# Query and key stacks turned by DMA instead of TensorE, the attention's early steps moved forward in the hand-written order, and the output bias added later

## Chip, cores and metric

One core of one Trainium2 chip. The metric is the device time of one launch in microseconds (us), median over runs. Engines: PE (TensorE), DVE (VectorE), ACT (ScalarE), POOL (GpSimd), SP (SyncE, which issues every DMA of this kernel).

## What is computed

A vision-tower layer on x of shape 8 x 512 x 256 x 4, float32:

```
h = einsum('bhid,oi,od->bho', x, weighted_sum, weight)     # token mixing: 8 x 512 x 256
q, k, v = split(layernorm(h) @ qkv_w.T + qkv_b)            # 16 heads of 16
q, k = unit(rotate(q)), unit(rotate(k))                    # rotary, then each head's row over its norm
h = h + softmax(q k' / 4) v @ out_w.T + out_b
p = sigmoid(layernorm(h) @ Wg + bg); w = p * (p > 0.5)     # 8 experts, each of 256 -> 1024 -> 256
h = h + sum_e w_e * (relu(layernorm(h) @ W1_e + b1_e) @ W2_e + b2_e)
```

## The kernel before

Eight batches of 512 tokens (four tiles of 128) run one after the other. The attention of batch 0 runs **alone**; then the experts (FFN) of batch b are **merged** with the attention of batch b+1, for b = 0 (where the expert weights are also split into two float16 parts and written to DRAM) and in a loop over b = 1 to 6; the experts of batch 7 end the program.

**FFN chunks.** An expert has 8 chunks of 128 hidden units, 64 chunks in all. Chunk c on PE is `f1 c` (6 matmuls of 128x512 into one of two PSUM banks, line 859) and, three chunks later (LAG), `f2 c` (12 matmuls of 128x256, lines 878 to 881). Between them ACT applies the ReLU twice (lines 666, 669), POOL forms the low part (line 549). `f1 n` waits for ACT's chunk n-2. After an expert's last `f2` DVE adds the result into `acc` (line 1091, "acc"); the next expert's first `f2` waits for that (line 874), since it reuses the banks.

**Order.** Each engine runs one fixed list, in order. `attention_order` (lines 56 to 88) gives every attention step a place counted in chunks, and `merge` (lines 112 to 133) puts the steps between the `f1` and `f2` of the chunks. The same step name is run by all the engines that have a part in it, so the place orders PE, ACT, DVE and POOL alike. In a chunk c the steps placed below c + 0.5 come after `f1 c`, then comes `f2 c-3` (and "acc" after an expert's last one), then the steps placed below c + 1.

**Attention steps** per tile t: `split` (x into two parts, ACT and DVE), `mix` (24 matmuls), `ln1`, `ln1_turn`, `qkv` (12 matmuls; DVE copies out with the bias, lines 963, 964), `rotate` (ACT squares at line 618, POOL at line 556, DVE at lines 976 to 982), `qk_norm` (DVE, 12 small operations per half, lines 989 and 894 to 901), `unit` (DVE, line 996), `stack` and `qk_turn`; then `scores`, `weigh` and the rest.

`stack t` writes the unit queries and keys as float16 high and low parts into one buffer `stack` (128 partitions x 2 x 1024): ACT the high (line 624), DVE the low (line 1005), for a = 0 (queries) and 1 (keys). `qk_turn t` transposes it on PE, 8 blocks of 128x128 for each a (line 761), into PSUM; ACT copies that into `qt` and `kt` (`take_turned`, line 588, traced at line 581, inside the next tile's `stack`). As there is one buffer, `stack t+1` on ACT and DVE waits until tile t has been turned (lines 622, 1004).

**SP's queue** is one list too. For expert e of batch b (`load_expert`, lines 489 to 496): wait for `f1` of expert e-2 to be done, load w1s (1 MB); wait for `f2` of expert e-2 to be done, load w2s (1 MB). For e = 3 the second wait is for `f2 15`:

```
wait(sp, f2_done, b, HM * (e - 1))
sp.dma_start(w2s[s][:], w2_parts[e]).then_inc(w2_in[s].sem, 16)
```

**The output bias** is added to `resid` by POOL (line 569) after the last `qkv`; `project`, after all scores, waits for it.

Of the kernel before, what the change touches and what calls it, by code (L numbers as in the profile page):

```python
# [26 lines left out]
P = 128  # L27
# [28 lines left out]
def attention_order(alone=False):  # L56
# [3 lines left out]
    for t in range(TT):  # L60
        steps += [(MIX[t - 1] - 0.05 if t else 0.3, "split", t), (MIX[t], "mix", t),
                  (9.0 + 1.5 * t, "ln1_turn", t), (10.55 + 1.5 * t, "qkv", t), (10.6 + 1.5 * t, "rotate", t),
                  (17.1 + 1.5 * t, "unit", t), (18.6 + 1.5 * t, "stack", t), (20 + 1.5 * t, "qk_turn", t)]
    steps += [(6.8, "ln1", 0), (14.7, "qk_norm", 0), (19.2, "qk_norm", 1)]
    if alone:

        order = ["ln1_turn 0", "ln1_turn 1", "qkv 0", "rotate 0", "ln1_turn 2", "qkv 1", "rotate 1", "qk_norm 0",
                 "unit 0", "ln1_turn 3", "qkv 2", "stack 0", "rotate 2", "unit 1", "qkv 3", "qk_turn 0", "stack 1",
                 "rotate 3", "qk_norm 1", "qk_turn 1", "unit 2", "stack 2", "unit 3", "qk_turn 2", "stack 3",
                 "qk_turn 3"]  # L70
        places = {name: 8 + 0.1 * k for k, name in enumerate(order)}
        steps = [(places.get(f"{stage} {n}", at), stage, n) for at, stage, n in steps]
# [19 lines left out]
MIX = [2.1, 3.5, 4.9, 6.3]  # L92
# [104 lines left out]
def build(nc, x_t, mix_w, mix_sum_t, qkv_w_t, qkv_b, out_w_t, out_b, gate_w, gate_b, w1, b1_t, w2, b2,  # L197
# [5 lines left out]
    with ExitStack() as ctx:  # L203
# [14 lines left out]
        ident16 = sb("ident16", [P, P], F16)  # L218
# [122 lines left out]
        stack_turned = signal("stack_turned", 2 * TT)  # L341
        qt_out = signal("qt_out", TT)
        kt_out = signal("kt_out", TT)
# [101 lines left out]
        def _(sp):  # L445
# [90 lines left out]
            with sp.Fori(1, BATCHES - 2) as i:  # L536
                body(i, True, True)
# [5 lines left out]
        def _(pool):  # L543
            def steps(stage, n, fb, ab):
# [21 lines left out]
                elif stage == "qkv" and n == TT - 1:  # L566
# [8 lines left out]
            pool.tensor_copy(ident16[:], ident[:]).then_inc(pool_consts, 1)  # L575
# [3 lines left out]
        def _(act):  # L579
            def copy(out_ap, in_ap):  # L580
                return act.activation(out_ap, in_ap, ACT.Copy)  # L581

            def take_turned(t, a, b, alone):

                dst, done = ((qt, qt_out), (kt, kt_out))[a]
                wait(act, stack_turned, b, 2 * t + a + 1)
                wait(act, scored, b, 0)
                copy(dst[:, :, t * P:(t + 1) * P], qk_turn_bank(a, alone)).then_inc(done.sem, 1)
# [9 lines left out]
            def steps(stage, n, fb, ab):  # L598
# [87 lines left out]
        def _(pe):  # L686
# [17 lines left out]
            def steps(stage, n, fb, ab):  # L704
# [46 lines left out]
                elif stage == "qk_turn":  # L751
                    if fb is not None:
                        wait(pe, qkv_out, ab, 2 * TT)
                    if n == 0 and fb is None:
                        pe.wait_ge(pool_consts, 2)
                    for a in range(2):
                        wait(pe, stack_ready, ab, 2 * n + a + 1)
                        wait(pe, (qt_out, kt_out)[a], ab, n)
                        turned = qk_turn_bank(a, fb is None)
                        for h in range(HEADS // 2):  # L760
                            last = pe.transpose(turned[:, h, :],  # L761
                                                stack[:, a, 2 * h:2 * h + 2, :, :].rearrange("p h s d -> p (h s d)"),
                                                ident16[:])
                        last.then_inc(stack_turned.sem, 1)
# [125 lines left out]
        def _(dve):  # L890
# [23 lines left out]
            def steps(stage, n, fb, ab):  # L914
# [281 lines left out]
```

## Time and profile before

| | us |
|---|---|
| median of 3 runs (lowest, highest) | 2021.08 (2020.14, 2027.73) |
| profiled execution: its own time, its span | 2029.17, 2027.4 |
| one turn of the merged loop (start of one f1 0 to the next) | 237.7 |
| experts of batch 7 alone, to the end | 173.3 |
| PE busy | 1911.6 (94%) |
| DVE, ACT, POOL busy | 792.3, 1142.6, 678.6 |

A row of a timeline has start, duration, engine, line, operation, output <- input, and in brackets the idle time of the engine before it and what ended that. Matmuls overlap, so starts tell their rate better than durations.

### The profile page before, as it was taken

To read this page: it belongs to the slowest core of one execution; us is meant where nothing else is said; L and a number is where in the kernel's file an instruction comes from. 1 tells how busy PE (TensorE), PEld (TensorE's weight loads), DVE (VectorE), ACT (ScalarE), POOL (GpSimd) and SP (SyncE) were. 2 spreads that over 40 slices of the span, in tenths; PEclk is the share of its full clock that TensorE was granted. 3 is DMA by queue.
4 is the path that set the end of the run, shared out by engine and by line. 5 is a ranking of instruction groups with operands and counts; after the bars stand their busy time and mean duration, and the time that the engine had idled before them with its cause. 6 is when DMAs were issued, how large, how long until landed. Compare 5 with 4: busy or idle time off the path is not lost.

```text
span 2027.4 us, 36619 instructions
## 1 busy us (share of the span) xinstructions
PE 1911.6 (94%) x13152; PEld 1211.9 (60%) x13152; DVE 792.3 (39%) x1660; ACT 1142.6 (56%) x1969; POOL 678.6 (33%) x570
## 2 busy tenths in 40 slices
PE   5679888899999999999999999999999999999999
PEld 4246543577547764567646675467655776456666
DVE  6756933547203380145602472133810456013000
ACT  2644666544765457644765447654576446754444
POOL 1103422324323242333423343232423334233443
PEclk8779999999999999999999999999999999999999
DMA  4113332332112221131212312122221322113221
GB/s 154 38 53 113 105 130 84 123 138 84 63 64 105 97 83 63 66 130 67 84 63 87 113 66 81 63 105 95 72 75 63 109 91 84 63 63 103 104 96 53
DMA packets 40461, 176.92 MB, mean 87 GB/s; under 512 B 4056, under 2 KB 17120, under 8 KB 23904
## 3 DMA queue, kind: packets, MB, share of 16 engines
q1 hardware_dynamic: 40288, 174.52, 24.2%
q8 instruction: 120, 1.97, 0.4%
q14 instruction: 53, 0.43, 0.1%
HBM read 153.54 MB, written 20.97 MB: 86 GB/s over the span
## 4 chain that ended last, share of the span: by engine, by line
PE 77%; issue 7%; DVE 7%; ACT 2%; POOL 1%; ACTq 0%; DVEq 0%; POOLq 0%
PE bank_h L859 28%; PE bank_f L878 10%; PE bank_f L880 10%; PE bank_f L881 10%; PE bank_o L788 5%; PE bank_s L776 3%; PE bank_s L692 2%; PE bank_s L693 2%; PE bank_s L694 2%; DVE tmp_b L976 1%; PE bank_s L761 1%; POOL hl L549 1%; DVE y L899 1%; PE bank_s L842 1%; ACT hh L669 1%
## 5 line engine op out<-in xcount | busy, mean ns | idle before, releaser
L549 POOL TENSOR_TENSOR hl<-h,hh 128x512 f16<-128x512 f32 x512 | 608.4, 1189 | 1148.2 <-ACT hh L669 670.7
L859 PE MATMUL bank_h<-x,w1s 128*128 128x512 f16 x3072 | 756.0, 383 | 19.5 <-issue 9.1
L666 ACT ACTIVATE h<-bank_h,b1s 128x512 f32<-128x512 f32 x512 | 353.5, 690 | 468.6 <-PE bank_h L859 452.7
L878 PE MATMUL bank_f<-w2s,hh 128*128 128x256 f16 x2048 | 563.2, 275 | 2.1 <-DVE acc L1091 1.3
L880 PE MATMUL bank_f<-w2s,hh 128*128 128x256 f16 x2048 | 561.1, 274 | 0.0
L881 PE MATMUL bank_f<-w2s,hl 128*128 128x256 f16 x2048 | 560.9, 274 | 0.0
L859 PEld LDWEIGHTS bank_h<-x,w1s 128*128 128x128 f16 x3072 | 287.6, 99 | 345.7 <-issue 49.9
L669 ACT ACTIVATE hh<-bank_h,b1s 128x512 f16<-128x512 f32 x512 | 352.7, 689 | 0.0
L636 ACT ACTIVATE probs<-bank_s 128x512 f32<-128x512 f32 x480 | 262.3, 604 | 153.7 <-PE bank_s L776 153.6
L878 PEld LDWEIGHTS bank_f<-w2s,hh 128*128 128x128 f16 x2048 | 202.2, 99 | 113.8 <-issue 41.0
L1091 DVE SCALAR_TENSOR_TENSOR acc<-bank_f,gw,acc 128x256 f32<-128x256 f32 x256 | 106.1, 476 | 349.9 <-PE bank_f L881 349.8
L880 PEld LDWEIGHTS bank_f<-w2s,hh 128*128 128x128 f16 x2048 | 201.6, 98 | 48.7 <-issue 0.8
L881 PEld LDWEIGHTS bank_f<-w2s,hl 128*128 128x128 f16 x2048 | 201.4, 98 | 24.4
L1009 DVE RECIPROCAL rc<-bank_m 128x16 f32<-128x16 f32 x32 | 8.2, 257 | 402.6 <-PE bank_m L798 402.6
L788 PE MATMUL bank_o<-probs,v 128*32 128x512 f32 x1024 | 137.2, 608 | 1.2 <-ACT probs L636 0.6
L776 PE MATMUL bank_s<-qt,kt 64*128 64x512 f16 x480 | 98.8, 392 | 15.0 <-ACT probs L636 13.6
L692 PE MATMUL bank_s<-mix,xh 128*128 128x256 f32 x256 | 78.0, 305 | 16.5 <-DVE xl L922 16.4
L776 PEld LDWEIGHTS bank_s<-qt,kt 64*128 64x128 f16 x480 | 24.4, 93 | 101.5 <-ACT probs L636 51.1
L922 DVE TENSOR_TENSOR xl<-xraw,xh 128x512 fp32r<-128x512 f32 x64 | 48.7, 772 | 83.3 <-ACT xh L581 83.3
L618 ACT ACTIVATE probs<-qk 128x512 f32<-128x512 f32 x32 | 20.2, 630 | 104.0 <-DVE qk L963 104.0
L556 POOL TENSOR_TENSOR tmp_a<-qk,cos 128x512 f32<-128x512 f32 x32 | 42.4, 1326 | 96.6 <-DVE qk L963 96.6
L693 PE MATMUL bank_s<-mix,xh 128*128 128x256 f32 x256 | 74.0, 289 | 0.0
(137 smaller groups left out, 1788.8 us busy)
## 6 DMA issues: line engine op xcount, KB each, us to landing
w1s<-w_parts SPq DMA_DIRECT2D x56, 1024.0 KB, 4.8
w2s<-w_parts SPq DMA_DIRECT2D x56, 1024.0 KB, 4.8
xraw<-in_x_t_dram SPq DMA_DIRECT2D x32, 512.0 KB, 4.1
raw<-in_w_dram SPq DMA_DIRECT2D x16, 1024.0 KB, 6.4
w_parts<-w1s SPq DMA_DIRECT2D x8, 1024.0 KB, 8.8
w_parts<-w2s SPq DMA_DIRECT2D x8, 1024.0 KB, 10.7
out_dram<-acc SPq DMA_DIRECT2D x16, 256.0 KB, 6.1
raw<-in_qkv_w_t_dram SPq DMA_DIRECT2D x1, 768.0 KB, 6.8
```

The source lines that it names most:

```text
L549: pool.tensor_tensor(hl[n % HBUFS][:], h32[n % 2][:], hh[n % HBUFS][:], ALU.subtract)\
L636: act.activation(probs[u % 2][:, 2 * half + j, :], score_bank(2 * n + j, fb is None)[:, :], ACT.Exp, scale=SCORE_SCALE).then_inc(exped.sem, 1)
L666: act.activation(h32[n % 2][:], bank_h[n % 2][:, :], ACT.Relu, bias=b1s[:, e, m:m + 1]).then_inc(h_hi.sem, 1)
L669: act.activation(hh[n % HBUFS][:], bank_h[n % 2][:, :], ACT.Relu, bias=b1s[:, e, m:m + 1]).then_inc(h_hi.sem, 1)
L692: pe.matmul(out_ap, high[k], w[k], start=start and k == 0, stop=False, skip_group_check=True)
L693: pe.matmul(out_ap, high[k], lo_w[k], start=False, stop=False, skip_group_check=True)
L776: pe.matmul(score_bank(2 * n + j, fb is None)[:, :], kt[lo:lo + 64, h // 2, tile * P:(tile + 1) * P], qt[lo:lo + 64, h // 2, :], start=Tru ...
L788: last = pe.matmul(bank_o[32 * j:32 * j + 32, :], v1[:, tile, h, :, :].rearrange("p s d -> p (s d)"), probs[n % 2][:, j, :], start=(tile = ...
L859: last = pe.matmul(bank_h[n % 2][:, :], w[:, wp, k, m * P:(m + 1) * P], x16[:, xp, k, :], start=(k == 0 and wp + xp == 0), stop=(k == DK - ...
L878: pe.matmul(o, high, w[:, 0, m, :], start=(m == 0 and t % 2 == 0), stop=False, skip_group_check=True)
L880: pe.matmul(o, high, w[:, 1, m, :], start=False, stop=False, skip_group_check=True)
L881: last = pe.matmul(o, low, w[:, 0, m, :], start=False, stop=(m == HM - 1), skip_group_check=True)
```

## The change

1. `qk_turn`, `take_turned`, `ident16` and the signals `qt_out` and `kt_out` are gone. SP issues eight DMA transposes per batch instead (`turn_stacks`), each from one half of `stack` (128 x 1024 float16, 256 KB) into 128 columns of `qt` or `kt`, after `stack_ready`. `stack_turned` becomes one semaphore for each of a = 0 and 1, raised by the DMA. In SP's list they come after `load_expert(b, 3)`; for batch 1 ahead of `load_raw(4)`; for batch 0 ahead of `load_raw(1)`.
2. Places: `mix` and `split` of tiles 1 to 3 1.1 chunks earlier, `ln1` to `rotate` 1.1, `qk_norm` 1.8 and 3.5, `unit` 1.9, `stack` 2.0. `scores` stays at 25.6.
3. The output bias is a step of its own at 23.5.
4. SP's loop over batches is unrolled.

```
-                  (9.0 + 1.5 * t, "ln1_turn", t), (10.55 + 1.5 * t, "qkv", t), (10.6 + 1.5 * t, "rotate", t),
-                  (17.1 + 1.5 * t, "unit", t), (18.6 + 1.5 * t, "stack", t), (20 + 1.5 * t, "qk_turn", t)]
-    steps += [(6.8, "ln1", 0), (14.7, "qk_norm", 0), (19.2, "qk_norm", 1)]
+                  (7.9 + 1.5 * t, "ln1_turn", t), (9.45 + 1.5 * t, "qkv", t), (9.5 + 1.5 * t, "rotate", t),
+                  (15.2 + 1.5 * t, "unit", t), (16.6 + 1.5 * t, "stack", t)]
+    steps += [(5.7, "ln1", 0), (12.9, "qk_norm", 0), (15.7, "qk_norm", 1), (23.5, "out_bias", 0)]
...
-MIX = [2.1, 3.5, 4.9, 6.3]
+MIX = [1.0, 2.4, 3.8, 5.2]
...
+            def turn_stacks(b, tiles):
+                for t in tiles:
+                    for a in range(2):
+                        wait(sp, stack_ready, b, 2 * t + a + 1)
+                        if t == 0:
+                            wait(sp, scored, b, 0)
+                        sp.dma_start_transpose((qt, kt)[a][:, :, t * P:(t + 1) * P],
+                                               stack[:, a].rearrange("p h s d -> p (h s d)"))\
+                          .then_inc(stack_turned[a].sem, 16)
...
             load_x(1, [0, 1])
+            turn_stacks(0, range(TT))
             load_raw(1)
...
             for e in range(2, EXPERTS):
+                if e == 3:
+                    turn_stacks(1, range(TT))
                 if e + 1 < EXPERTS:
                     load_raw(e + 1)
...
                 for e in range(2, EXPERTS):
                     load_expert(b, e)
+                    if more and e == 3:
+                        turn_stacks(b + 1, range(TT))
...
-            with sp.Fori(1, BATCHES - 2) as i:
+            for i in range(1, BATCHES - 2):
                 body(i, True, True)
...
-                elif stage == "qkv" and n == TT - 1:
+                elif stage == "out_bias":
                     wait(pool, ln1_out, ab, TT)
                     pool.tensor_tensor(resid[:], resid[:], outb[:].unsqueeze(1).broadcast_to([P, TT, D]),
...
                 elif stage == "stack":
                     wait(act, qk_unit, ab, n + 1)
                     for a in range(2):
-                        wait(act, stack_turned, ab, 2 * (n - 1) + a + 1)
+                        wait(act, stack_turned[a], ab, 16 * n)
                         high, _, unit_qk = stack_slots(n, a)
                         copy(high, unit_qk).then_inc(stack_hi.sem, 1)
-                        if n:
-                            take_turned(n - 1, a, ab, fb is None)
...
                         wait(dve, stack_hi, ab, 2 * n + a + 1)
-                        wait(dve, stack_turned, ab, 2 * (n - 1) + a + 1)
+                        wait(dve, stack_turned[a], ab, 16 * n)
                         dve.tensor_tensor(low, unit_qk, high, ALU.subtract).then_inc(stack_ready.sem, 1)
```

## Rows read from the trace of the kernel before

**Rows 1.** Stages: us, each engine's busy us (instructions), granted clock (PEclk), DMA share, GB/s.
```profile
903.00:1140.60 237.60, 233.30 (x1646) 148.07 (x1645) 88.25 (x191) 138.47 (x242) 83.57 (x69) 1.00 0.23 83
...
940.00:965.00 25.00, 25.00 (x165) 18.34 (x164) 16.87 (x26) 11.46 (x21) 12.21 (x10) 1.00 0.13 52
...
218.00:222.00 4.00, 1.66 (x4) 0.58 (x5) 3.97 (x6) 2.94 (x5) 2.90 (x3) 0.72 0.05 20
```

**Rows 2.** Waits of PE in one turn of the merged loop: total, times, longest.
```profile
PE bank_h L859 <- ACT hh L669: 1.0, 1, 1.0
PE bank_s L761 <- issue: 0.5, 1, 0.5
PE bank_s L692 <- DVE xl L922: 0.5, 1, 0.5
```

**Rows 3.** The chain of waits in that turn: start, us, what.
```profile
980.06 1.30 PE bank_h L859 x6
981.36 0.89 PE bank_s L761 x16
```

**Rows 4.** ACT's copies of the turned keys: busy, mean ns | idle.
```profile
L581 ACT ACTIVATE kt<-bank_s 128x1024 f16<-128x1024 f16 x28 | 29.5, 1054 | 0.0
```

**Rows 5.** Timeline in that turn: the bias on POOL, and what ran beside and after it.
```profile
967.13 2.34 POOL L569 TENSOR_TENSOR resid<-resid,outb 128x1024 f32<-128x1024 f32 x1
...
967.25 2.30 DVE L899 SCALAR_TENSOR_TENSOR y<-y 128x64 f32<-128x64 f32 x1
...
970.11 0.22 DVE L899 SCALAR_TENSOR_TENSOR y<-y 128x64 f32<-128x64 f32 x1
...
974.23 1.47 PE L859 MATMUL bank_h<-x,w1s 128*128 128x512 f16 x6 [1.03 <-ACT hh L669]
```

**Rows 6.** PE at the start of that turn: three f1, then the first mix.
```profile
908.18 4.37 PE L859 MATMUL bank_h<-x,w1s 128*128 128x512 f16 x18 [1.81 <-issue]
913.05 0.36 PE L692 MATMUL bank_s<-mix,xh 128*128 128x256 f32 x1 [0.50 <-DVE xl L922]
```

**Rows 7.** SP's issues and PE around f2 15.
```profile
977.04 0.32 SPq L496 DMA_DIRECT2D w2s<-w_parts  x1
...
978.45 0.28 PE L878 MATMUL bank_f<-w2s,hh 128*128 128x256 f16 x1
```

**Rows 8.** DVE in that turn, from tile 2's qkv to the second qk_norm.
```profile
960.67 0.69 DVE L963 TENSOR_TENSOR qk<-bank_s,qkvb 128x512 f32<-128x512 f32 x1 [1.27 <-PE bank_s L694]
...
976.56 1.05 DVE L996 TENSOR_TENSOR probs<-qk,y 128x512 f32<-128x512 f32 x1
977.53 1.65 DVE L1091 SCALAR_TENSOR_TENSOR acc<-bank_f,gw,acc 128x256 f32<-128x256 f32 x4
...
980.90 1.19 DVE L989 TENSOR_SCALAR ss<-ss 128x64 f32<-128x64 f32 x1
...
985.91 1.29 DVE L1005 TENSOR_TENSOR stack<-probs,stack 128x512 f16<-128x512 f32 x2
```

**Rows 9.** DMA issues by line: times, KB each, us to landing (first row: 976 to 984 us alone).
```profile
w2s<-w_parts SPq DMA_DIRECT2D x1, 1024.0 KB, 4.7
...
w_parts<-w2s SPq DMA_DIRECT2D x8, 1024.0 KB, 10.7
```

**Rows 10.** Landing times of the DMAs of L476, of L480 and of L502.
```profile
DMA to landing us min/median/max: 4.7/4.8/6.0
...
DMA to landing us min/median/max: 6.7/6.8/7.5
...
DMA to landing us min/median/max: 2.1/6.1/7.6
```

**Rows 11.** Timeline of batch 0's attention, alone: the last stack and the first scores.
```profile
72.08 0.63 ACT L581 ACTIVATE stack<-probs 128x512 f16<-128x512 f32 x1 [0.45 <-DVE probs L996]
...
77.36 0.61 PE L776 MATMUL bank_s<-qt,kt 64*128 64x512 f16 x2 [1.16 <-issue]
```

**Rows 12.** PE's timeline with batch 0's experts: the first f1 after a gap.
```profile
220.34 2.74 PE L859 MATMUL bank_h<-x,w1s 128*128 128x512 f16 x6 [2.81 <-ACT hh L669]
```

More of the change, by code:

```diff
@@ L61, in attention_order @@
         steps += [(MIX[t - 1] - 0.05 if t else 0.3, "split", t), (MIX[t], "mix", t),
-                  (9.0 + 1.5 * t, "ln1_turn", t), (10.55 + 1.5 * t, "qkv", t), (10.6 + 1.5 * t, "rotate", t),
-                  (17.1 + 1.5 * t, "unit", t), (18.6 + 1.5 * t, "stack", t), (20 + 1.5 * t, "qk_turn", t)]
-    steps += [(6.8, "ln1", 0), (14.7, "qk_norm", 0), (19.2, "qk_norm", 1)]
+                  (7.9 + 1.5 * t, "ln1_turn", t), (9.45 + 1.5 * t, "qkv", t), (9.5 + 1.5 * t, "rotate", t),
+                  (15.2 + 1.5 * t, "unit", t), (16.6 + 1.5 * t, "stack", t)]
+    steps += [(5.7, "ln1", 0), (12.9, "qk_norm", 0), (15.7, "qk_norm", 1), (23.5, "out_bias", 0)]
     if alone:
         order = ["ln1_turn 0", "ln1_turn 1", "qkv 0", "rotate 0", "ln1_turn 2", "qkv 1", "rotate 1", "qk_norm 0",
-                 "unit 0", "ln1_turn 3", "qkv 2", "stack 0", "rotate 2", "unit 1", "qkv 3", "qk_turn 0", "stack 1",
-                 "rotate 3", "qk_norm 1", "qk_turn 1", "unit 2", "stack 2", "unit 3", "qk_turn 2", "stack 3",
-                 "qk_turn 3"]
+                 "unit 0", "ln1_turn 3", "qkv 2", "stack 0", "rotate 2", "unit 1", "qkv 3", "stack 1",
+                 "rotate 3", "qk_norm 1", "unit 2", "stack 2", "unit 3", "stack 3"]
         places = {name: 8 + 0.1 * k for k, name in enumerate(order)}
@@ L217, in build @@
         ident = sb("ident", [P, P])
-        ident16 = sb("ident16", [P, P], F16)
         mix = sb("mix", [P, 2, XK, D], F32R)
@@ L340, in build @@
         stack_ready = signal("stack_ready", 2 * TT)
-        stack_turned = signal("stack_turned", 2 * TT)
-        qt_out = signal("qt_out", TT)
-        kt_out = signal("kt_out", TT)
+        stack_turned = [signal(f"stack_turned{a}", 16 * TT) for a in range(2)]
         scored = signal("scored", 4 * UNITS)
@@ L387, in qkv_banks @@
             return bank_h if alone and t % 2 else bank_s
-        def qk_turn_bank(a, alone):
-            return (bank_f if alone else bank_s)[a][:, :].bitcast(F16).rearrange("p (h t) -> p h t", t=P)
         def stack_slots(t, a):
@@ L574, in _ @@
             pool.wait_ge(consts_in, 16 * 9)
-            pool.tensor_copy(ident16[:], ident[:]).then_inc(pool_consts, 1)
             run(pool, steps)
@@ L581, in copy @@
                 return act.activation(out_ap, in_ap, ACT.Copy)
[L583 to L588, printed above, removed]
             def split_x(b, t):
@@ L621, in steps @@
                     for a in range(2):
-                        wait(act, stack_turned, ab, 2 * (n - 1) + a + 1)
+                        wait(act, stack_turned[a], ab, 16 * n)
                         high, _, unit_qk = stack_slots(n, a)
                         copy(high, unit_qk).then_inc(stack_hi.sem, 1)
-                        if n:
-                            take_turned(n - 1, a, ab, fb is None)
-                elif stage == "qk_turn" and n == TT - 1:
-                    for a in range(2):
-                        take_turned(n, a, ab, fb is None)
                 elif stage == "scores":
@@ L750, in steps @@
                     last.then_inc(qkv_done.sem, 1)
[L751 to L764, printed above, removed]
                 elif stage == "scores":
@@ L767, in steps @@
                     if n == 0:
-                        wait(pe, qt_out, ab, TT)
-                        wait(pe, kt_out, ab, TT)
+                        for turned in stack_turned:
+                            wait(pe, turned, ab, 16 * TT)
                         wait(pe, qkv_out, ab, 2 * TT)
@@ L783, in steps @@
                         wait(pe, ln1_lo, ab, TT)
+                        if fb is None:
+                            pe.wait_ge(pool_consts, 1)
                     if tile == 0:
```

## The prediction, made before the changed kernel ran

> **What bounds the kernel now.** I read the stages first. In a turn of the merged loop PE is busy 233.3 of 237.6 us at the full granted clock (PEclk 1.00 is the level of 2.4 GHz), DVE, ACT and POOL for 88, 138 and 84 [rows 1]. So PE's own work is the turn, and an edit there pays in two ways only: work that leaves PE, or a wait of PE that appears or goes. The waits of PE come next: beside the start of a turn they are 1.0 us for ACT's ReLU, 0.5 at the first turning on PE and 0.5 for the split of x [rows 2]. From 940 to 965 us PE never waits [rows 1]. An engine off PE matters only where PE's next instruction stands behind it, and so the lists of DVE, ACT and SP around `f2 15` decide this change.
>
> **The turnings on PE.** The 16 blocks of a tile take 0.89 us in the chain of waits, an `f1` 1.30 [rows 3]. Four tiles: 3.6 us, and the 0.5 us wait before one of them [rows 2]: -4.1 us a turn.
>
> **ACT's copies.** 8 per batch of 1.05 us [rows 4] go. PE waits for none of them [rows 2], so I cost this at 0.
>
> **The bias.** POOL's addition takes 2.34 us, and beside it one small DVE operation takes 2.30 us where the same operation 3 us later takes 0.22 [rows 5]. DVE thus loses 2.1 us inside `qk_norm 0`, behind it stand DVE's `qkv 3` copy, ACT's square and ReLU, and PE's `f1 18` waits 1.03 us for that ReLU [rows 5, 2]. At 23.5 DVE has nothing beside it but the end of `stack 3`. On POOL it then stands before chunk 24's `hl`, which `f2 24` needs three chunks later; that cover is 3 x 2.6 us against 2.34. Without it 2 us would come back. -1.0 us a turn.
>
> **`mix` earlier.** Now PE runs three `f1` and then waits 0.5 us for the split of x [rows 6]. In the new order `mix 0` stands after two, while the split still follows ACT's first ReLU, so it is ready at the same time: PE waits one `f1` longer, +1.3 us a turn. Later `mix` steps have a chunk of slack, and I see no wait of PE in which the 1.3 could vanish. `split 1` passes ACT's second ReLU, which `f1 3` needs only after `mix 1`: 0. Bounds 0 and 1.8 (all of the wait).
>
> **`ln1` to `rotate` earlier.** PE has no wait there [rows 1] and the order among these steps stays, so 0. One neighbour changes: DVE's accumulate after `f2 7` now follows `rotate 0`; I count about 1 us of slack before `f2 8`. If it is gone, 1 us.
>
> **The new wait.** Call the end of `f2 15` E. Before, SP issues w2s right behind it (977.04, so E is about 976.85), and `f2 16` starts at E + 1.6, after `f1 19` [rows 7]. The places give this new list in chunk 18: `f1 18`, `stack 1`, `unit 2`, then `f2 15` and its accumulate. Before, the accumulate came ahead of `stack 0`. So on DVE the accumulate for which `f2 16` waits now stands behind `stack 1`, and `stack 1` on ACT and DVE waits until tile 0 has been turned. SP issues those DMAs only after the wait of `load_expert(b, 3)` for `f2 15`, and behind its 1 MB. No edge goes round in a circle, but the chain is: end of `f2 15`, w2s, two turned stacks, ACT, DVE, `f2 16`.
> - Is tile 0's stack ready by then? Before, DVE runs from tile 2's `qkv` copy (960.67) to `unit 0` (976.56) without much rest, 15.9 us [rows 8]. New: 15.9 - 2.1 (bias) + 1.05 (`unit 0`) + 5.0 (`qk_norm 1`, from 980.90 to 985.91, now ahead of `stack 0`) + 1.3 (the two low parts) = 21.2 us. PE from the same point to E: 16.2 before; three half chunks more (3.9) and 1.0 of waiting less give 19.1. So the stack is ready at E + 2, and w2s, which lands 4.7 us after its issue [rows 9], at E + 4.9. The transfers come behind it in the same queue.
> - One turned stack is 256 KB. The trace has no such DMA. Lower end: the plain rate; the shortest store of 256 KB (L502) lands after 2.1 us [rows 10] and w2s with four times as much after 4.7, so (4.7 - 2.1) / 3 = 0.9 us for each 256 KB more. Upper end: the slowest large DMA, 10.7 us [rows 9]. Between: the loads of L476 and L480 both move 1 MB, in 256 runs of 4 KB and 1024 runs of 1 KB by their code, and land after 4.8 and 6.8 us [rows 10]; 768 runs more cost 2.0 us. A stack cut into blocks of 128 columns is 1024 runs of 256 bytes, the stored 256 KB are 256 runs of 1 KB. So 0.9 + 2.0 = 2.9 us, an estimate, and I take it: these loads are the rows nearest in what a turning multiplies, the runs.
> - The two stacks land at E + 7.8 and E + 10.7. Then ACT's copy 0.63 [rows 11], DVE's low part 0.65, `unit 2` 1.05, half of the accumulate 0.8 [rows 8]: `f2 16` at E + 13.8, against E + 1.6: +12.2 us. At 0.9 us a stack it is +8.2.
> - Behind it: after an idle of 2.81 us one `f1` takes 2.74 us instead of the 1.46 of one without a gap [rows 12, 5] and that stage has a granted clock of 0.72 [rows 1], which is part of it spent at 1.2 GHz. +1.3 us.
> - Later tiles: a pair every 5.8 us (2 x 2.9) lands tile 3 at E + 28.1; PE gets to `scores 0` after 7 chunks of 2.6 us and the stall, E + 30.4. No further wait. What SP holds back meanwhile, w1s of expert 4, is needed 8 chunks after its old issue: 0. SP's unrolled loop and PE's wait at `weigh`: 0, both wait for others anyway.
>
> The Trainium skill prices the stack twice. *DMA: Bandwidth & Descriptors*, section Latency and other measured facts, gives a DMA transpose 261 GB/s; that makes 1.0 us a stack, an estimate, and a sum of about 2058. *VectorE: DVE Perf Modes*, section The three transpose paths, gives 1309 ns for one 128x128 block by DMA against 390 for TensorE; eight blocks in a row would be 10.5 us, an estimate, and the sum that of the slow rival below. The trace's 16 blocks in 0.89 us [rows 3] are 56 ns each on PE, far below the page's 390, and no run here shows the DMA yet.
>
> **The sum.** A turn: +12.2 + 1.3 + 1.3 - 4.1 - 1.0 = +9.7, six turns: +58. Batch 1's attention has no w2s ahead of its DMAs but the same accumulate behind `stack 1`, and DVE is busier there; it also loses the bias's wait and the gap that follows (2.81 and 1.28 us [rows 12]): I put +2 (-4 to +12). Batch 0: tiles 2 and 3 follow each other at once, 5.3 us from the last stack to the scores [rows 11]; two landings of about 4 us in place of PE and ACT: +5 (0 to 12). In all +65. The profiled execution took 2029.2 us, 8 above the median of the three runs; the turns are alike in both, so I add to the median: 2021 + 65 = **2086**.
>
> **Rivals.**
> - *Short transfers* (0.9 us a stack): +5.7 a turn, and +1 in all outside the turns: 2021 + 34 + 1 = 2056. For it: the same bytes as any copy. Against: the run count.
> - *Slow transfers.* A stack takes as long as the slowest large DMA, 10.7 us [rows 9]. Then pairs are what the batch waits for: tile 3 lands at E + 4.9 + 8 x 10.7 = E + 90 where `scores 0` stood at E + 18: +72, less 4 saved, seven batches, and some 40 us more in batch 0: about 2540. From about 5 us a stack on (pairs at 10 us, +26 a turn at `scores`) it passes 2200. For it: nothing in the trace; against it: the rows from which I took 2.9.
> - *No stall, so faster.* The place is the accumulate after `f2 15`. If the second stack lands by E + 2.3, `f2 16` is late by less than the 3.8 us that the rest of a turn gains (4.1 + 1.0 - 1.3), and if it lands early enough nothing is lost: 2021 - 6 x 3.8 - 5 = 1993, or 1985 if the `mix` wait is absorbed too. It needs DVE to have `stack 0` ready before `f2 15` and the DMAs not to queue behind w2s. For it: w2s could be overtaken, and PE's work does fall by 4.1. Against it: SP's own order, which I read from the code.
> - *Given back evenly.* The DMAs don't wait for w2s and are short: the second stack lands 2.1 us after it is ready, at E + 4.1, `f2 16` is 5.6 late, less 5.1, and with or without the `mix` wait it ends between 2011 and 2031.
>
> **Chances.** The forecast's case (1.5 to 5 us a stack) 0.45, short 0.18, slow (over 5) 0.12, given back 0.11, faster 0.14. Slower by over 0.5% (10 us, about what a measurement of this kernel can tell): 0.45 + 0.18 + 0.12 = 0.75; within it 0.11; faster 0.14. The range of 2005 to 2200 leaves out the slow rival's upper part (0.10) and most of the faster case (0.10).
>
> **What would show it.** Right: in the waits of PE a wait of 8 us or more, once a turn, at L878 for DVE's accumulate or for `stack`; DVE's low part of `stack 1` waiting for a DMA into `qt` or `kt`; landing times that start behind w2s; PE busy down by 4 us a turn, the bias beside no DVE operation, 1.8 us before `mix 0`. Wrong: the turn below 237 us with no such wait; a wait at `scores` or in ACT's ReLU as the largest; or transfers of other than 1.5 to 5 us each.

## The result, and the profile after

The changed kernel takes 2071.73 us (median of 4 runs, 2066.59 to 2073.78), the kernel before 2024.07 beside it (4 runs): a ratio of 1.0232, 95% interval 1.0209 to 1.0255. The forecast was 2086, with 0.75 for slower: the direction and the range held, and the rise came out at 47.7 us where the working had 65.

The profiled executions span 2070.3 and 2027.4 us. DVE's copy of x marks the start of each turn: from the second copy to the eighth it was 430.5 to 1853.9 us before and is 433.1 to 1896.9 now. So the six turns hold 40.4 of the 42.9 us (237.2 us a turn became 244.0), what lies ahead of them 2.6, the last experts nothing.

In the changed kernel `f1` is L842, `f2` L861 to L864, the mix L687, the scores L757, the accumulate L1074, the split of x L905, the stack's copy L588 (ACT) and low part L988 (DVE), `unit` L979, the transposes L497. First the windows, as in [rows 1]: two turns, and three short stretches inside turns.

```profile
675.80:918.50 242.70, 230.02 (x1582) 145.34 (x1580) 83.14 (x192) 131.97 (x234) 83.03 (x69) 0.99 0.28 90
918.50:1163.50 245.00, 232.18 (x1582) 146.73 (x1580) 82.99 (x191) 132.08 (x234) 82.73 (x69) 0.97 0.27 89
685.00:689.00 4.00, 3.66 (x28) 3.29 (x29) 1.49 (x3) 1.16 (x2) 0.00 (x0) 1.00 0.46 142
928.00:932.00 4.00, 3.93 (x23) 3.96 (x24) 1.22 (x2) 0.63 (x1) 0.00 (x0) 0.67 0.48 136
1003.70:1008.00 4.30, 4.30 (x17) 2.46 (x18) 2.68 (x5) 1.26 (x2) 0.27 (x1) 0.52 0.54 122
```

PE runs 64 instructions fewer in a turn (the turnings), and is idle 12.7 us of it where it was 4.3 [rows 1]. Its busy time falls from 233.3 to 230.0 in one turn and only to 232.2 in the other, by the granted clock: 0.99 against 0.97. The waits of PE in the first of these turns, to be read against [rows 2]:

```profile
PE bank_f L861 <- DVE acc L1074: 8.6, 1, 8.6
PE bank_s L687 <- DVE xl L905: 2.1, 1, 2.1
PE bank_h L842 <- issue: 1.9, 1, 1.9
```

The last line was there before. The 1.0 us for the ReLU behind the bias and the 0.5 at the first turning are gone, the 0.5 before the mix is 2.1, and one wait is new: `f2 16` for DVE's accumulate. The timeline of the next turn around that wait, the stretch of [rows 7, 8]; a line of dots stands for rows left out:

```profile
993.48 1.46 PE L842 MATMUL bank_h<-x,w1s 128*128 128x512 f16 x6
...
993.68 0.32 SPq L488 DMA_DIRECT2D w2s<-w_parts  x1
...
993.96 2.13 DVE L988 TENSOR_TENSOR stack<-probs,stack 128x512 f16<-128x512 f32 x2
995.52 1.24 SPq L497 DMA_TRANSPOSE qt<-stack  x1
996.02 0.68 DVE L979 TENSOR_TENSOR probs<-qk,y 128x512 f32<-128x512 f32 x1
996.86 2.01 SPq L497 DMA_TRANSPOSE kt<-stack  x1
999.98 0.63 ACT L588 ACTIVATE stack<-probs 128x512 f16<-128x512 f32 x1 [6.34 <-DMA qt<-stack]
1000.80 1.43 DVE L988 TENSOR_TENSOR stack<-probs,stack 128x512 f16<-128x512 f32 x2 [4.10 <-ACT stack L588]
1000.87 0.63 ACT L588 ACTIVATE stack<-probs 128x512 f16<-128x512 f32 x1 [0.27 <-DMA kt<-stack]
...
1001.52 1.23 SPq L497 DMA_TRANSPOSE qt<-stack  x1
...
1002.14 0.68 DVE L979 TENSOR_TENSOR probs<-qk,y 128x512 f32<-128x512 f32 x1
1002.74 1.65 DVE L1074 SCALAR_TENSOR_TENSOR acc<-bank_f,gw,acc 128x256 f32<-128x256 f32 x4
...
1003.67 0.40 PE L861 MATMUL bank_f<-w2s,hh 128*128 128x256 f16 x1 [8.73 <-DVE acc L1074]
```

Read it from the bottom. `f2 16` starts when DVE has accumulated half of `f2 15`; DVE stands first at `stack 1`, which waits 4.10 us for ACT, and ACT waited 6.34 us for the first transpose of tile 0 to land; SP issued that one behind w2s. `f2 15` ended at E = 993.5, so `f2 16` is at E + 10.2, and then runs at 0.52 of the full clock for 4.3 us (window above). The DMA view of the whole run:

```profile
DMA packets 108038, 193.59 MB, mean 94 GB/s; under 512 B 71640, under 2 KB 84704, under 8 KB 91488
...
w2s<-w_parts SPq DMA_DIRECT2D x56, 1024.0 KB, 4.8
qt<-stack SPq DMA_TRANSPOSE x32, 2.7
kt<-stack SPq DMA_TRANSPOSE x32, 2.8
```

A transpose of 256 KB lands 2.7 to 2.8 us after its issue (median), 4.5 and 4.0 us in the stretch above, behind w2s.

### The profile page after: what moved, and what is told of

It is laid out like the page before. It is cut to its first block, busy times and chain, and to the rows that moved or that the text cites. A ratio compares the mean times of both kernels' runs of the same rounds, so it can differ in the third digit from the quotient of the medians.

```text
span 2070.3 us, 35350 instructions
## 1 busy us (share of the span) xinstructions
PE 1890.8 (91%) x12640; PEld 1190.9 (58%) x12640; DVE 758.5 (37%) x1660; ACT 1089.7 (53%) x1905; POOL 671.4 (32%) x569
## 2 busy tenths in 40 slices
DMA packets 108038, 193.59 MB, mean 94 GB/s; under 512 B 71640, under 2 KB 84704, under 8 KB 91488
## 4 chain that ended last, share of the span: by engine, by line
PE 78%; DVE 6%; issue 6%; ACT 2%; POOL 1%; DMA 1%; SPq 0%; DVEq 0%; ACTq 0%; POOLq 0%
PE bank_h L842 29%; PE bank_f L861 10%; PE bank_f L863 10%; PE bank_f L864 10%; PE bank_o L771 5%; PE bank_s L757 3%; PE bank_s L687 3%; PE bank_s L689 3%; PE bank_s L688 3%; DMA kt<-stack 1%; ACT hh L664 1%; PE bank_s L825 1%; POOL hl L557 1%; PE bank_m L781 1%; DVE qk L964 1%
## 5 line engine op out<-in xcount | busy, mean ns | idle before, releaser
L557 POOL TENSOR_TENSOR hl<-h,hh 128x512 f16<-128x512 f32 x512 | 600.4, 1173 | 1236.1 <-ACT hh L664 669.1
L842 PE MATMUL bank_h<-x,w1s 128*128 128x512 f16 x3072 | 762.1, 386 | 11.9 <-issue 9.8
L861 PE MATMUL bank_f<-w2s,hh 128*128 128x256 f16 x2048 | 567.2, 277 | 64.8 <-DVE acc L1074 64.0
L863 PE MATMUL bank_f<-w2s,hh 128*128 128x256 f16 x2048 | 565.4, 276 | 0.0
L864 PE MATMUL bank_f<-w2s,hl 128*128 128x256 f16 x2048 | 565.1, 276 | 0.0
L842 PEld LDWEIGHTS bank_h<-x,w1s 128*128 128x128 f16 x3072 | 290.8, 99 | 339.1 <-issue 58.3
L861 PEld LDWEIGHTS bank_f<-w2s,hh 128*128 128x128 f16 x2048 | 203.2, 99 | 179.4 <-DVE acc L1074 55.2
L1074 DVE SCALAR_TENSOR_TENSOR acc<-bank_f,gw,acc 128x256 f32<-128x256 f32 x256 | 106.1, 477 | 365.0 <-PE bank_f L864 364.9
L863 PEld LDWEIGHTS bank_f<-w2s,hh 128*128 128x128 f16 x2048 | 202.6, 99 | 51.9 <-issue 0.8
L864 PEld LDWEIGHTS bank_f<-w2s,hl 128*128 128x128 f16 x2048 | 202.6, 99 | 25.9
L757 PE MATMUL bank_s<-qt,kt 64*128 64x512 f16 x480 | 98.0, 393 | 34.1 <-DMA kt<-stack 22.3
L687 PE MATMUL bank_s<-mix,xh 128*128 128x256 f32 x256 | 81.3, 318 | 28.8 <-DVE xl L905 28.8
L757 PEld LDWEIGHTS bank_s<-qt,kt 64*128 64x128 f16 x480 | 24.0, 93 | 120.5 <-issue 70.0
L588 ACT ACTIVATE stack<-probs 128x512 f16<-128x512 f32 x64 | 38.5, 627 | 90.2 <-DMA qt<-stack 56.2
L905 DVE TENSOR_TENSOR xl<-xraw,xh 128x512 fp32r<-128x512 f32 x64 | 50.9, 807 | 87.7 <-ACT xh L588 87.6
L988 DVE TENSOR_TENSOR stack<-probs,stack 128x512 f16<-128x512 f32 x64 | 55.4, 888 | 69.4 <-ACT stack L588 68.3
L689 PE MATMUL bank_s<-mix,xl 128*128 128x256 f32 x256 | 77.3, 302 | 0.0
```

The lines of the kernel that those rows point to most:

```text
L557: pool.tensor_tensor(hl[n % HBUFS][:], h32[n % 2][:], hh[n % HBUFS][:], ALU.subtract)\
L687: pe.matmul(out_ap, high[k], w[k], start=start and k == 0, stop=False, skip_group_check=True)
L689: last = pe.matmul(out_ap, low[k], w[k], start=False, stop=stop and k == n - 1, skip_group_check=True)
L757: pe.matmul(score_bank(2 * n + j, fb is None)[:, :], kt[lo:lo + 64, h // 2, tile * P:(tile + 1) * P], qt[lo:lo + 64, h // 2, :], start=Tru ...
L842: last = pe.matmul(bank_h[n % 2][:, :], w[:, wp, k, m * P:(m + 1) * P], x16[:, xp, k, :], start=(k == 0 and wp + xp == 0), stop=(k == DK - ...
L861: pe.matmul(o, high, w[:, 0, m, :], start=(m == 0 and t % 2 == 0), stop=False, skip_group_check=True)
```

## The experiments

The theory: the time is lost at `f2 16`, because tile 1's stack waits for tile 0's transposes ahead of the accumulate, and a little at the mix. Rivals: the transposes themselves are slow or disturb the weights; or the order costs the same without them. Ratios are to the kernel before, timed beside each; they stand as recorded, and a quotient of two medians differs from them by up to 0.002.

### The parts of the change, undone one at a time

**The mix back by a chunk.**

```diff
-MIX = [1.0, 2.4, 3.8, 5.2]
+MIX = [2.0, 3.1, 4.2, 5.2]
```

> The changed kernel with one edit: the mixes stand at 2.0, 3.1, 4.2 and 5.2, so that the first again follows three f1 instead of two, while the last keeps its new place. Theory (the changed kernel's added time is the accumulate of expert 1 held behind stack 1, plus PE's longer wait at the first mix, plus lost clock): PE's wait at L687 for the split falls from 2.1 to 0.5 us a turn and the stage's granted clock stays at 1.00, so 1.6 us a turn and up to 0.9 more where the clock fell; with batch 1, 10 to 18 us less than the changed kernel, a ratio to the kernel before of 1.015 to 1.019 where the changed kernel has 1.023. Rival (the time of the first mix is absorbed by PE's longer wait later): no difference, 1.022 to 1.025.

Ratio 1.0153 (1.0134 to 1.0172), a turn of 242.1 us. PE's waits in a turn of this kernel:

```profile
PE bank_f L861 <- DVE acc L1074: 8.7, 1, 8.7
...
PE bank_s L687 <- DVE xl L905: 0.5, 1, 0.5
```

The mix waits 0.5 us again, and the large wait is untouched. So the mix's place costs 1.8 us a turn, 1.6 of it waiting. Behind the mix the granted clock now stays at 1.00 in all six turns, where it fell in four; but PE's busy time falls by only 0.3 us a turn (231.6 to 231.3), since the slow stretch behind `f2 16` remains.

**The stacks two chunks apart.**

```diff
-                  (15.2 + 1.5 * t, "unit", t), (16.6 + 1.5 * t, "stack", t)]
+                  ([15.2, 16.7, 18.6, 20.7][t], "unit", t), ([16.6, 18.55, 20.6, 22.6][t], "stack", t)]
```

> The changed kernel with one edit: stack 1 and unit 2 move from 18.1 and 18.2 to 18.55 and 18.6, behind f2 15 and its accumulate on DVE, and the later units and stacks are spread out (unit 3 at 20.7, stacks 2 and 3 at 20.6 and 22.6). Theory (the accumulate waits behind stack 1, which waits for the turned tile): f2 16 then waits only for DVE's backlog, about 2.7 us instead of 8.7, with some 1 to 3 us of new waits at f1 21 to f1 24 for ACT, which still waits for the tiles; with less clock lost about 4 to 6 us a turn less, ratio 1.004 to 1.012. Rival (the wait for the turned tile itself costs the time, wherever it stands, as ACT and its ReLU stand behind it too): the waits move to f1 and the ratio stays within 1.018 to 1.026.

Ratio 1.0045 (1.0029 to 1.0060), a turn of 237.8 us. In a turn of this kernel the wait shrinks from 8.7 to 2.6 us, and little new appears (0.9 us for the ReLU in three of the six turns):

```profile
PE bank_f L861 <- DVE acc L1074: 2.6, 1, 2.6
```

With the accumulate ahead of `stack 1` most of the loss is gone, and every transpose is still there. So the transfers as such cost little; what costs is that the accumulate stands behind `stack 1`. Whether that is the wait for the landing or DVE's own work there, this run does not separate, as both moved; the second buffer below does.

**Tile 0's transposes ahead of w2s** on SP:

```diff
+                if e == 3 and b + 1 < BATCHES:
+                    turn_stacks(b + 1, [0])
...
-                        turn_stacks(b + 1, range(TT))
+                        turn_stacks(b + 1, range(1, TT))
```

> The changed kernel with one edit: SP issues tile 0's two transposes after w1s of expert 3 and ahead of its wait for f2 15 and of w2s; the other tiles stay. Theory (DVE's backlog makes tile 0's stack ready only 2 us after f2 15, and w2s in front adds the rest): the two land 2.7 us after they are issued instead of 4.5 and 4.0, so stack 1 and with it the accumulate come about 1.3 us earlier, f2 16 waits some 7.4 us; 1 to 2 us a turn less, ratio 1.016 to 1.021. Rival (the queue behind w2s is most of the wait): f2 16 waits under 5 us, ratio below 1.012.

Ratio 1.0164 (1.0141 to 1.0187); in a turn of this kernel (`f2` is L863) the wait is 7.5 us instead of 8.6 or 8.7:

```profile
PE bank_f L863 <- DVE acc L1076: 7.5, 1, 7.5
```

The queue behind the 1 MB load is about 1.1 us of it.

**The bias later, on the kernel before.**

```diff
-    steps += [(6.8, "ln1", 0), (14.7, "qk_norm", 0), (19.2, "qk_norm", 1)]
+    steps += [(6.8, "ln1", 0), (14.7, "qk_norm", 0), (19.2, "qk_norm", 1), (23.5, "out_bias", 0)]
...
-                elif stage == "qkv" and n == TT - 1:
+                elif stage == "out_bias":
```

> The kernel before with one edit: the output bias is a step at 23.5 instead of following the last qkv. Theory: DVE's slow small operation of 2.30 us beside the bias goes, with it PE's wait of 1.0 us at f1 18 and some of the 0.9 us before f2 16, and in batch 1 a wait of 2.8 us with its slow f1; 1.0 to 1.9 us a turn and about 4 us in batch 1, 10 to 16 us in all, ratio 0.992 to 0.995. Rival (DVE is late for other reasons, and PE's wait only moves): ratio 0.998 to 1.001.

Ratio 0.9953 (0.9937 to 0.9969), a turn of 236.1 us, 1.1 less. This part of the change pays as forecast.

### The DMA alone, and the order alone

**The transposes by DMA, with the places, mix and bias of before.**

```diff
-                  (7.9 + 1.5 * t, "ln1_turn", t), (9.45 + 1.5 * t, "qkv", t), (9.5 + 1.5 * t, "rotate", t),
-                  (15.2 + 1.5 * t, "unit", t), (16.6 + 1.5 * t, "stack", t)]
-    steps += [(5.7, "ln1", 0), (12.9, "qk_norm", 0), (15.7, "qk_norm", 1), (23.5, "out_bias", 0)]
+                  (9.0 + 1.5 * t, "ln1_turn", t), (10.55 + 1.5 * t, "qkv", t), (10.6 + 1.5 * t, "rotate", t),
+                  (17.1 + 1.5 * t, "unit", t), (18.6 + 1.5 * t, "stack", t)]
+    steps += [(6.8, "ln1", 0), (14.7, "qk_norm", 0), (19.2, "qk_norm", 1)]
...
-MIX = [1.0, 2.4, 3.8, 5.2]
+MIX = [2.1, 3.5, 4.9, 6.3]
...
-                elif stage == "out_bias":
+                elif stage == "qkv" and n == TT - 1:
```

> The change's first part alone: DMA transposes in SP's list as in the changed kernel, but the places and the bias of the kernel before, so that the accumulate of expert 1 stays ahead of stack 0 and the first mix follows three f1. Theory (the cost lies in the places, not in the DMA): a pair lands some 4 us after its first half is ready, tiles follow each other every 5.5 us, and tile 3 lands about when its copies by ACT were done before; PE loses no more than 1 us a turn at f1 or scores and saves 4.1: 15 to 30 us less than the kernel before, ratio 0.985 to 0.993. Rival (the DMA's latency itself costs, wherever the stacks stand): PE waits 4 us or more a turn at scores or f1, ratio 1.000 or more.

Ratio 1.0051 (1.0032 to 1.0071), a turn of 240.0 us: the theory missed, its rival was nearer. The timeline of one turn of this kernel, the last chunks before the scores:

```profile
990.86 2.29 DVE L988 TENSOR_TENSOR stack<-probs,stack 128x512 f16<-128x512 f32 x2
...
992.57 1.23 SPq L497 DMA_TRANSPOSE qt<-stack  x1
...
995.29 0.63 ACT L588 ACTIVATE stack<-probs 128x512 f16<-128x512 f32 x1 [4.62 <-DMA qt<-stack]
...
996.67 0.63 ACT L588 ACTIVATE stack<-probs 128x512 f16<-128x512 f32 x1 [0.75 <-DMA kt<-stack]
...
997.78 0.68 ACT L664 ACTIVATE hh<-bank_h,b1s 128x512 f16<-128x512 f32 x1
...
998.51 2.12 PE L842 MATMUL bank_h<-x,w1s 128*128 128x512 f16 x6 [3.17 <-ACT hh L664]
...
1004.06 1.23 SPq L497 DMA_TRANSPOSE kt<-stack  x1
...
1006.97 0.39 PE L757 MATMUL bank_s<-qt,kt 64*128 64x512 f16 x2 [1.40 <-issue]
```

It is the wait for a landing again, in another place. `stack 1` is done at 993; ACT stands 4.62 and 0.75 us at the copy for `stack 2`, and the experts' ReLU behind it makes PE wait 3.17 us. The last transpose is issued at 1004.06, 2.9 us before the scores start. With one buffer the next tile's pair is issued 4.2 us or more after a tile's, in this kernel and in the changed one (here at 992.57 and 996.83), and the old places leave the last tiles too little time for it.

**Wider places with the old early part**, an attempt to cure that (the lines against the run just above):

```diff
-                  (17.1 + 1.5 * t, "unit", t), (18.6 + 1.5 * t, "stack", t)]
-    steps += [(6.8, "ln1", 0), (14.7, "qk_norm", 0), (19.2, "qk_norm", 1)]
+                  ([16.6, 18.1, 20.1, 22.1][t], "unit", t), ([17.6, 19.5, 21.4, 23.3][t], "stack", t)]
+    steps += [(6.8, "ln1", 0), (14.7, "qk_norm", 0), (19.52, "qk_norm", 1)]
```

> The DMA transposes with the old early part (old mix, old input norm, old bias), and only the units, stacks and the second half of the query and key norms put elsewhere: units at 16.6, 18.1, 20.1, 22.1, stacks at 17.6, 19.5, 21.4, 23.3, the second half of the norm at 19.52, just behind stack 1. Theory (the transpose's time costs PE only where the next stack is due before it has landed, because ScalarE then waits in order with the experts' activations queued behind that wait): with two chunks between stacks the two waits of f1 on ScalarE (1.05 and 3.17 us in a turn of the run with the old places), the half clock behind them and most of the 1.4 us at the first scores go, so a turn of 240.0 us becomes about 234 to 235 and the whole run 0.985 to 0.995 of before. Rival (a DMA transpose between two TensorE stages costs its landing wherever it stands, or the 67,000 added packets slow the weights): no turn below 237, ratio 1.000 or more.

Ratio 1.0121 (1.0088 to 1.0153), a turn of 240.0 us: a miss. PE's waits in a turn of this kernel:

```profile
PE bank_f L861 <- DVE acc L1074: 3.0, 1, 3.0
PE bank_s L757 <- issue: 2.1, 1, 2.1
...
PE bank_h L842 <- ACT hh L664: 1.0, 1, 1.0
```

PE waits at `f2` for the accumulate behind `stack 1`, at the scores, and for the ReLU. With the early part where it was, the first stack is ready at 980 and the last transpose is issued at 999.32, 2.9 us before the scores at 1002.21. So this spacing moved the loss and did not cure it; other spacings were not tried. The better version below has the early part ahead.

**The order of the change, turnings on PE** (new lines only; the bias becomes a step as in its own run above):

```diff
+                  (7.9 + 1.5 * t, "ln1_turn", t), (9.45 + 1.5 * t, "qkv", t), (9.5 + 1.5 * t, "rotate", t),
+                  (15.2 + 1.5 * t, "unit", t), (16.6 + 1.5 * t, "stack", t), (18 + 1.5 * t, "qk_turn", t)]
+    steps += [(5.7, "ln1", 0), (12.9, "qk_norm", 0), (15.7, "qk_norm", 1), (23.5, "out_bias", 0)]
...
+MIX = [1.0, 2.4, 3.8, 5.2]
```

> The change's other parts alone: the kernel before with the changed kernel's places, mixes and bias, the turning still on PE, 1.4 chunks behind each stack as before (18.0 to 22.5). Theory (the order itself holds the accumulate of expert 1 behind qk_norm 1, stack 0 and stack 1, and the first mix behind two f1): PE waits some 3 us for DVE's stack before the first turning and 2 to 4 us before f2 16, plus 1.6 at the first mix, and gains 1.0 by the bias: 4 to 8 us a turn more, ratio 1.010 to 1.025. Rival (only the DMA's landing makes the wait; the order alone is harmless): ratio 0.993 to 1.003.

Ratio 1.0187 (1.0157 to 1.0216), a turn of 242.2 us. PE's waits in a turn of this kernel (L761 turns, L692 mixes):

```profile
PE bank_s L761 <- issue: 2.2, 1, 2.2
...
PE bank_s L692 <- DVE xl L922: 2.1, 1, 2.1
PE bank_s L761 <- DVE stack L1005: 0.9, 1, 0.9
```

No transpose is moved by DMA here, and 5.0 us of a turn are lost all the same, where the change loses 6.7: `qk_norm 1` now stands ahead of `stack 0`, and PE stands at the turning instead of at `f2 16` (2.2 us, by the code for DVE's first low part of `stack 0`, and 0.9 for the second). Most of the loss of the change is thus its order.

### A second stack buffer

The stack's buffer is what makes tile 1 wait for tile 0. Two of them by turns, each with its own count of landings, take that reason away:

```diff
-        stack = sb("stack", [P, 2, HEADS, 4, HD], F16)
+        stacks = [sb(f"stack{k}", [P, 2, HEADS, 4, HD], F16) for k in range(2)]
...
-                        wait(act, stack_turned[a], ab, 16 * n)
+                        wait(act, stack_turned[a][n % 2], ab, 16 * (n // 2))
...
-                        wait(dve, stack_turned[a], ab, 16 * n)
+                        wait(dve, stack_turned[a][n % 2], ab, 16 * (n // 2))
```

**In the changed kernel:**

> The changed kernel with its places, mix and bias, and one thing else: two stack buffers by turns (tiles 0 and 2, tiles 1 and 3), each with its own count of landings, so that a tile's stack waits for the transposes of the tile two before it. Theory (the stall before f2 16 is the one stack buffer: ScalarE and VectorE wait for the landing of tile 0 before they may write tile 1, and the experts' accumulation stands behind that wait): of the 64.0 us on eight waits of f2 for the accumulation at most 2 us each stay, the half clock behind them goes too, 9.5 to 12 us of each of eight stalls, ratio 0.975 to 0.988. Rival (VectorE's order, or the transposes' packets beside the weights, holds f2 16): the waits stay over 5 us each and the ratio over 1.005.

Ratio 1.0110 (1.0091 to 1.0129), a turn of 240.6 us: the theory missed by more than half. The timeline of one turn of this kernel, from `qk_norm 1` on DVE to `f2 16` (`f2 15` ends at 985.3):

```profile
980.72 1.15 DVE L972 TENSOR_SCALAR ss<-ss 128x64 f32<-128x64 f32 x1
...
985.61 2.25 DVE L988 TENSOR_TENSOR stack<-probs,stack 128x512 f16<-128x512 f32 x2
...
987.78 0.68 DVE L979 TENSOR_TENSOR probs<-qk,y 128x512 f32<-128x512 f32 x1
...
988.49 1.15 ACT L588 ACTIVATE stack<-probs 128x512 f16<-128x512 f32 x2 [3.04 <-DVE probs L979]
...
989.21 1.29 DVE L988 TENSOR_TENSOR stack<-probs,stack 128x512 f16<-128x512 f32 x2 [0.75 <-DVE probs L979]
...
990.42 0.69 DVE L979 TENSOR_TENSOR probs<-qk,y 128x512 f32<-128x512 f32 x1
...
991.02 1.65 DVE L1074 SCALAR_TENSOR_TENSOR acc<-bank_f,gw,acc 128x256 f32<-128x256 f32 x4
...
991.95 0.40 PE L861 MATMUL bank_f<-w2s,hh 128*128 128x256 f16 x1 [5.20 <-DVE acc L1074]
```

Up to `f2 16` neither DVE nor ACT waits for a DMA now (ACT does so once behind it, 1.9 us at `stack 2`), and `f2 16` still comes 5.2 us late: DVE works through `qk_norm 1`, `stack 0`, `unit 1`, `stack 1` and `unit 2` before the accumulate. The landing is the other 3.5 of the 8.7 us.

**In the DMA alone:**

> The DMA transposes alone (old places, old mix, old bias, ratio 1.0051 with one stack buffer) with two stack buffers by turns. Theory (what made the DMA alone slower was that one buffer passes from tile to tile in 4.3 us or more, so that the last tiles' stacks came at the scores with the experts' activations behind them on ScalarE): the waits of f1 on ScalarE, 28.6 us on 14 in that run, fall to about the 9.0 of before, and the 1.4 us at the first scores by half; a turn of 240.0 us becomes 233 to 235.5, ratio 0.978 to 0.993. Rival (the landing of the last tile itself is too late for the scores in the old places, two buffers or one): the wait at the scores grows to 3 us or more and the ratio stays at 1.000 or above.

Ratio 0.9979 (0.9966 to 0.9992), a turn of 237.1 us: between the two. PE's waits in a turn of this kernel:

```profile
PE bank_s L757 <- DMA kt<-stack: 2.1, 1, 2.1
PE bank_h L842 <- ACT hh L664: 1.6, 2, 1.0
```

The ReLU's 4.2 us a turn fall to 1.6, less far than the theory had it: in the whole run 28.6 us became 15.8, not 9.0. The last landing holds the scores for 2.1, as the rival said, though it had 3 or more. Those 2.1 us, the ReLU's 0.6 above the 1.0 of before, and a lower clock (busy 229.4 us in the two turns at 1.00, 230.9 in the mean) take back about the 4.1 us that the turnings gave.

### A better version

**All three repairs together** (mix, places, tile 0 ahead of w2s), and `qk_norm 1` behind `stack 1`:

```diff
-    steps += [(5.7, "ln1", 0), (12.9, "qk_norm", 0), (15.7, "qk_norm", 1), (23.5, "out_bias", 0)]
+    steps += [(5.7, "ln1", 0), (12.9, "qk_norm", 0), (18.57, "qk_norm", 1), (23.5, "out_bias", 0)]
```

> The changed kernel with the edits of the first three experiments together, and one more: the second qk_norm moves from 15.7 to 18.57, so that on DVE stack 0, unit 1, the accumulate of expert 1 and stack 1 come ahead of it. Theory: what is left of the wait at f2 16 (2.6 us a turn with stack 1 alone moved, DVE's backlog) goes, the first mix waits 0.5 us and no clock is lost; a turn then is that of the kernel before less 4.1 (turnings on PE), 1.0 (bias) and 0.5 to 0.9 (its wait before f2 16), some 232 us; seven batches save 35 to 40 us, batch 0 gives back 2 to 3: ratio 0.981 to 0.986. Rival (the transposes hold ACT and DVE up somewhere else as soon as one wait is closed): a new wait of PE of 2 us or more at f1 or at scores, ratio above 0.990.

Ratio 0.9855 (0.9829 to 0.9882), a turn of 233.2 us: faster than both kernels. (The profiled execution was the slowest of the five, 2007.7 us against a median of 1998.3, so its turn is on the long side.) PE waits 0.5 us at the mix and 1.4 to 1.7 for the ReLU in a turn.

**The same order with the turnings on PE**, each 1.4 chunks behind its stack (the lines of the order against the better version; SP moves no stack here):

```diff
-                  ([16.6, 18.55, 20.6, 22.6][t], "stack", t)]
+                  ([16.6, 18.55, 20.6, 22.6][t], "stack", t),
+                  ([18.0, 19.95, 22.0, 24.0][t], "qk_turn", t)]
```

> TensorE turns the stacks as before, with everything else as in the best version with DMA transposes: the early part a chunk or two ahead, the mix at 2.0, 3.1, 4.2, 5.2, the bias at 23.5, stacks at 16.6, 18.55, 20.6, 22.6 with each tile's turning 1.4 behind its stack. Theory (the DMA transposes are worth TensorE's 32 turnings of a turn, 3.5 to 4.1 us, and the order alone about nothing beyond the bias): a turn of 236 to 237.5 us against 233.2 with the DMA, ratio 0.993 to 1.001. Rival (the gain of the best version comes from the order, the mix and the bias, and the DMA brings none of it): ratio 0.985 to 0.990, as that version's 0.9855.

Ratio 0.9943 (0.9928 to 0.9959), a turn of 234.9 us. The intervals lie apart, so the DMA brings some 0.9% in this order. The better order alone brings no more than the bias does (0.9953).

**The better version with two stack buffers:**

> The best version so far (0.9855, stacks two chunks apart) with two stack buffers by turns. Theory: its places already give each tile time to land, and of its waits only f1 on ScalarE, 1.4 us in a turn, hangs on the one buffer; so it gains 0 to 1.4 us a turn, ratio 0.979 to 0.987. Rival (some of its time still hangs on the one buffer where the waits do not show it): under 0.978.

Ratio 0.9827 (0.9807 to 0.9846), median 1990.28 us, a turn of 231.4. Its interval overlaps that of one buffer, so the gain of the buffer here is not settled, though the 1.4 to 1.7 us for the ReLU are gone from the turns; against the kernel before it is 1.7%. One turn of this kernel in the windows, and its waits of PE:

```profile
653.90:885.10 231.20, 228.61 (x1582) 144.67 (x1581) 82.77 (x191) 131.44 (x234) 83.23 (x69) 1.00 0.29 94
```

```profile
PE bank_h L844 <- issue: 1.9, 1, 1.9
PE bank_s L689 <- DVE xl L907: 0.5, 1, 0.5
```

In this turn nothing that belongs to the change is waited for any more, and at the full clock PE's work is 228.6 us against 233.3 [rows 1]. The nine combinations side by side:

| order | turnings on PE | DMA, one buffer | DMA, two buffers |
|---|---|---|---|
| of before | 1 | 1.0051 | 0.9979 |
| of the change | 1.0187 | 1.0232 | 1.0110 |
| stacks two chunks apart, mix later, `qk_norm 1` behind `stack 1` | 0.9943 | 0.9855 | 0.9827 |

(The first row has the bias in its old place; in the last, tile 0's transposes go ahead of w2s.) Read down, the change's order costs 1.9% with the turnings on PE and 1.8% with the DMA and one buffer. Read across, the DMA with one buffer costs 0.4 to 0.5% in the first two orders and gains 0.9% in the last.

## Why the prediction was right, and where it was off

The place was right: one wait a turn, at `f2 16`, for the accumulate behind `stack 1`, behind the landing of tile 0, behind w2s on SP. Tile 0's stack was forecast ready at E + 2; its two low parts end 2.6 us after E.

**The step that failed is the price of a transpose**, "0.9 + 2.0 = 2.9 us, an estimate, and I take it". The count of runs was right: packets under 512 B grew from 4056 to 71640, 1056 for each of the 64 transposes, and 1024 were forecast. But they cost nothing like 2 us. The pair landed at E + 6.5 and E + 7.4 instead of E + 7.8 and E + 10.7, 0.9 us apart, and `f2 16` came at E + 10.2 instead of E + 13.8. The row of the loads (L476 and L480) was the wrong neighbour; those come from the chip's main memory and a transpose here goes from buffer to buffer, but whether that is why was not tried. The short rival's 0.9 us a stack was the right size, and put `f2 16` at E + 9.8. By the prediction's own list, transfers of other than 1.5 to 5 us each are a sign against its case: what came is *short transfers*, to which it gave 0.18 and 2056 us. A turn came out at +6.7, between that rival's +5.7 and the forecast's +9.7, and the clock cost 3.0 of it where both had 1.3. So the nearness of 2086 is in part luck: the transposes were put 3.6 us a turn too dear (12.2 against 8.6), the clock 1.7 too cheap. The Trainium skill's 261 GB/s (*DMA: Bandwidth & Descriptors*, section Latency and other measured facts), 1.0 us a stack as an estimate, agrees with the 0.9 us between the landings. The Trainium skill's 1309 ns for one block (*VectorE: DVE Perf Modes*, section The three transpose paths), taken eight times in a row, 10.5 us as an estimate, does not: eight blocks landed 2.7 us after issue, all overhead included.

**The stall's cause was given wholly to the transfers.** The working listed `stack 1`, `unit 2` and the accumulate behind each other on DVE, yet let the case without a stall be faster if only `stack 0` was ready before `f2 15` and nothing queued. The order without DMA (1.0187) and the second buffer (1.0110) show that 5.2 of the 8.7 us are DVE's own queue. So the faster rival would not have come even with transposes that take no time.

The other terms, per turn:

- PE's turnings: -4.1 forecast, right. In the better order PE is busy 232.2 us of a turn at the full clock with the turnings and 228.6 without, 3.6 less, which is four times 0.89 [rows 3]; and the 0.5 us wait went. From the kernel before to 228.6 it is 4.7, but the other 1.1 came without the DMA: 0.7 with the bias (232.6 at the full clock in the kernel before with the bias later), 0.4 not traced.
- ACT's copies: 0, right; ACT is 6.5 us less busy and nobody gains.
- Bias: -1.0 forecast, -1.1 alone on the kernel before.
- Mix: +1.3 forecast with 1.8 as its bound; the wait grew by 1.6.
- Clock: +1.3 forecast. The six turns' mean busy time is 231.6, 3.0 more than the 228.6 of the version without stalls. The forecast took one slow `f1` after a gap of 2.81 us [rows 12]. (What it calls an `f1` without a gap stands in [rows 5] behind 1.03 us of idle; it takes 1.47 us all the same.) In the turn shown more than 4 us ran at 0.52 after 8.7 us idle, and in four of the six turns the mix's wait had a slow stretch behind it as well.
- `ln1` to `rotate`: 0, right; no wait at `f2 8`.

Together, in means over the six windows: idle +8.4 (12.4 against 3.9), PE's work at the full clock -4.7, clock +3.0 make +6.7 a turn, where the forecast had +9.7. Batch 0 took 1.5 us more (+5 forecast), what follows up to the first turn 1.1 (+2 forecast for batch 1); the accumulate is waited for there too, once for 9.7 us, and what gave that back was not taken apart.

## What to carry to other kernels

When a step is moved ahead in a hand-made order, list what then stands behind it on each in-order engine, and ask for the first instruction there that the bound engine needs: here an accumulate behind two stacks cost more than the work that left PE. A transfer that replaces work on an engine needs its latency in the plan, from the source's last write to the landing: with the consumers two chunks apart the same DMA that lost here gained 0.9% with one buffer, and where they stood closer a second buffer gave back 0.7 to 1.2%.

## What the runs showed of the hardware

SP needs 1.23 to 1.36 us to issue most transposes of 256 KB, about four times the 0.32 of w2s's 1 MB; the second one behind w2s took 2.0 us, the longest 2.25.

The 67,584 added packets under 512 B left the median landing of w2s at 4.8 us in both kernels, but not that of the loads beside the transposes. The w2s just ahead of tile 0's landed after 5.2 to 5.4 us in the six turns (4.7 to 4.9 before), the w1s behind the last transpose after 5.1 to 5.5 (4.8 to 4.9 before in five turns, 6.2 in one). PE waited for neither. The w2s of the stretch above, to be read against [rows 9]:

```profile
w2s<-w_parts SPq DMA_DIRECT2D x1, 1024.0 KB, 5.3
```

An idle of 2.1 us at the mix left the granted clock at 1.00 in one turn and took it to 0.67 in the next (windows of 4 us above), with the same instructions before it; what decides between the two was not found.
